# Carried sums of an expert stage added onto the output by five GpSimd transfers between the scatters

## The chip, the cores and the metric

The kernel runs on one core of one Trainium2 chip. The metric is the device time of one execution in microseconds (us). The kernel before took 2507.95 us, the median of 3 runs that lie between 2502.75 and 2509.33.

## What is computed

One layer of a graph transformer on 6250 nodes of 256 features, all in f32. A graph attention part sums over 206250 edges, and a linear attention part runs over all nodes; both are added to the input. Then a mixture of experts follows: each node is sent to its two best of 8 experts (256 to 512 to 256, GELU), weighted by a softmax of the two scores, and added to the node's row. Cut to what matters here:

```python
    x = x + gnn(layernorm(x), edges) + mix(layernorm(x))
    # ffn, on the layer norm of the new x:
    logits = xn @ Wr + br
    top_vals, top_idx = jax.lax.top_k(logits, 2)
    w = softmax(top_vals)
    for e in range(8):
        h = gelu(xn @ W1[e] + b1[e])
        y = y + (h @ W2[e] + b2[e]) * w_full[..., e, None]
    x = x + y
```

## The kernel before

Nodes lie in 49 tiles of 128 rows. A main stage of about 2200 us gathers the rows of the edges' sources (L1262), block by block, and weaves the other parts in between. As soon as a group of tiles has its new rows x, they are stored to `out` and also sent, by expert, into a DRAM tensor `expert_in`. An expert tile is 256 such rows of one expert. The first 28 expert tiles ("carried") are worked off inside the main stage and leave their result rows in a DRAM tensor `y_rows`; `y_at` tells for each node and each of its two choices where its row lies in it (or a row of zeros).

`tail_stage` (L2165) is the last stage, some 290 us, and the change is in it alone. It has T = 28 expert tiles left. Each engine has a hand-written program; the order in which an engine's waits and instructions stand in it is the order in which it runs. Per tile n:

- SP loads the 256 rows (`rows_in`, L2270) and the two weight matrices of the tile's expert (`weights`, L2277 and L2278, 512 KB each), into 3 buffers each. The weights of tile n wait until `down(n - 3)` is done.
- PE transposes the rows (`rows_across`, L2380), multiplies by W1 (`up`, L2392) and by W2 (`down`, L2404), in the order up(n), rows_across(n+1), down(n-1).
- ACT applies GELU (L2359).
- DVE scales the transposed rows (`rows_back`, L2432 to L2436, L681, L682) and makes the result rows `ye` (`result`, L2448, L2450). The result of tile n-1 stands in turn n of DVE's loop. There are 6 buffers for `ye` and 9 for the row numbers.
- GpSimd (POOL) adds the 256 result rows onto `out` in DRAM by two indirect transfers with compute_op add, 128 rows each (`result`, L2327). Two adding transfers must not meet on one row, so each tile's pair waits on the semaphore `added` until the pair before has landed.

Beside the tiles, GpSimd fetches the rows of the carried tiles for the nodes of the first 35 node tiles: two indirect gathers for each node tile t (`early_rows`, L2317), the first choice into `early[t]`, the second into one of GS = 5 buffers `second`. DVE adds the second to the first (`early_sum`, L2453) and counts in `early_done`; the gather of node tile t waits until sum t - 4 is done, because it takes that buffer. Five node tiles are gathered ahead of the first scatter; the others follow in `TILES_AFTER`, one node tile after most scatters. DVE makes its first five sums in turn LAG - 1 = 3.

When all 28 tiles are scattered, an epilogue puts `early` onto the output in five groups of 7 node tiles (896 KB): SP reads the rows of `out` into SBUF (`sums`, L2302), DVE adds (L2480), ACT's queue stores them (L2368).

The stage also carries the last group of node tiles, three of them, through its row steps (`part`, a shared function with numbered steps u; `STEPS` gives each step's tile, the same for all engines): steps 4 to 9 give the new x (ACT scales h by a weight of each row and head, L386; DVE adds, L484, and takes reciprocals; ACT scales again, L395; DVE adds the base, L489), 10 to 12 the normalised rows, 13 to 20 the logits, 29 to 33 the choice and the places. Its rows are then scattered to `expert_in` (L344, `SENDS_AT`), and the tile list for tiles 11 to 27 is made (`tile_list`).

Of the kernel before, what the change touches and what calls it, by code (L numbers as in the profile page):

```python
# [20 lines left out]
P = 128  # L21
# [182 lines left out]
class Round:  # L204


    def __init__(self, i, k=0, t=0, l=0, s=0, m=0, turned=False, spread=False):
        self.first, self.gt = sum(SIZES[:i]), SIZES[i]
        self.k, self.t, self.l, self.s, self.m, self.turned, self.spread = k, t, l, s, m, turned, spread
# [22 lines left out]
def rows_part(g, sems, ps):  # L232
# [239 lines left out]
    def vector(dve, own, r, u):  # L472
# [7 lines left out]
        if u == 5:  # L480
            dve.wait_ge(dev_ready, 3 * r.k + 1)
# [5 lines left out]
        elif u == 7:  # L487
            dve.wait_ge(dev_ready, 3 * r.k + 2)
# [9 lines left out]
        elif u == 11:  # L498
            dve.wait_ge(dev_ready, 3 * r.k + 3)
# [93 lines left out]
def tile_list(dve, own, g, count, tiles, partial):  # L593
# [5 lines left out]
    own.do(dve.tensor_tensor(room[:, :], taken[0:1, :], cap[0:1, :], ALU.subtract))  # L599
    own.do(dve.tensor_scalar(room_i[:, :], room[:, :], float(MT - 1 if partial else 0), None, ALU.add))  # L600
    own.do(dve.tensor_scalar(room_i[:, :], room_i[:, :], MT.bit_length() - 1, None, ALU.arith_shift_right))
    own.do(dve.tensor_copy(room[:, :], room_i[:, :]))
    own.do(dve.tensor_tensor(room[:, :], room[:, :], done[:, :], ALU.subtract))
    own.do(dve.tensor_tensor_scan(upto[:, :], unit[:, :], room[:, :], 0.0, ALU.mult, ALU.add))

    own.do(dve.tensor_scalar(coef[:, :], room[:, :], float(-MT), float(CAP), ALU.mult, ALU.add))
    own.do(dve.scalar_tensor_tensor(out=coef[:, 0:E - 1], in0=done[:, 1:E], scalar=float(MT), in1=coef[:, 0:E - 1],
                                    op0=ALU.mult, op1=ALU.add))
    own.do(dve.scalar_tensor_tensor(out=coef[:, :], in0=done[:, :], scalar=float(-MT), in1=coef[:, :], op0=ALU.mult, op1=ALU.add))
# [12 lines left out]
    own.do(dve.tensor_tensor(done[:, 1:E], done[:, 1:E], upto[:, 0:E - 1], ALU.subtract))  # L622

# [1541 lines left out]
def tail_stage(nc, g):  # L2165
# [11 lines left out]
    GS = 5  # L2177
    AHEAD = 5
    LAG = 4
    GATHERS_IN = [2] * GATHERED_TILES  # L2180
    TILES_AFTER, at_tile = {}, AHEAD
    for n in range(REST - 2):
        work = 0
        most = 4 if n in (2, 5, 8, 11) else 2
        while at_tile < GATHERED_TILES and work + GATHERS_IN[at_tile] <= most:
            work += GATHERS_IN[at_tile]
            TILES_AFTER.setdefault(n, []).append(at_tile)
            at_tile += 1
# [4 lines left out]
    PADS_AT = max(STEPS) + 1  # L2193
# [10 lines left out]
    with ExitStack() as ctx:  # L2204
# [28 lines left out]
        second = after_rows(GS * DIM).rearrange("p (s d) -> p s d", s=GS)  # L2233
# [14 lines left out]
        y_in += [Since(old["mix_loads"], 16 * old["MIX_LOADS"]), Since(sem("y_in"), 0)]  # L2248
        early_done, sum_done = Since(old["gdiag"], 1), Since(old["smax_ready"], 1)
        sums = region[:, 0:GATHERED_TILES * DIM].rearrange("p (i t d) -> p i t d", t=GT, d=DIM)  # L2250
# [4 lines left out]
        out_done = Since(weights_in, 16)  # L2255
        xe_loads = [len(range(i, T, XS)) - (i < 2) for i in range(XS)]
        w_loads = [len(range(i, T, WS)) - (i < 1) for i in range(WS)]
        sums_in = [Since(xe_in[i], 16 * xe_loads[i]) for i in range(XS)]
        sums_in += [Since(w_in[i], 32 * w_loads[i]) for i in range(GATHERED_TILES // GT - XS)]
# [3 lines left out]
        def _(sp):  # L2263
# [35 lines left out]
            sp.wait_ge(added, 32 * T)  # L2299
            sp.wait_ge(ye_ready, T)  # L2300
            for i in range(GATHERED_TILES // GT):
                sp.dma_start(sums[:, i], out[i * GT * P:(i + 1) * GT * P, :].rearrange("(t p) d -> p t d", p=P)).then_inc(sums_in[i].sem, 16)  # L2302
            out_done.wait(sp, 16 * (GATHERED_TILES // GT))

        @block.gpsimd
        def _(pool):
# [5 lines left out]
            def early_rows(t):  # L2312

                if t >= GS:
                    early_done.wait(pool, t - GS + 1)
                for c in range(2 - GATHERS_IN[t], 2):
                    pool.indirect_dma_start(  # L2317
                        out=second[:, t % GS, :] if c else early[:, t, :], out_offset=None, in_=y_rows[:, :],
                        in_offset=bass.IndirectOffsetOnAxis(ap=y_at[:, c, t:t + 1], axis=0)).then_inc(y_in[t % GS].sem, 16)
# [10 lines left out]
            for t in range(AHEAD):  # L2330
                early_rows(t)
            for n in range(T):
# [6 lines left out]
                for t in TILES_AFTER.get(n, ()):  # L2339
# [3 lines left out]
        def _(act):  # L2343
            part.sums(act, last, range(G_HEADS // 2, G_HEADS))
# [8 lines left out]
            for n in range(T):  # L2353
# [8 lines left out]
                for u in STEPS.get(n, ()):  # L2362
# [3 lines left out]
            for i in range(GATHERED_TILES // GT):  # L2366
                sum_done.wait(act, i + 1)
                act.dma_start(out[i * GT * P:(i + 1) * GT * P, :].rearrange("(t p) d -> p t d", p=P),  # L2368
                              early[:, i * GT:(i + 1) * GT, :]).then_inc(out_done.sem, 16)

        @block.tensor
        def _(pe):
# [35 lines left out]
            for n in range(T):  # L2408
                up(n)
                if n + 1 < T:  # L2410
# [3 lines left out]
                for u in STEPS.get(n, ()):  # L2414
# [4 lines left out]
        def _(dve):  # L2419
# [6 lines left out]
            def rows_back(n):  # L2426
                e = dve.value_load(tile_expert[0:1, n:n + 1], min_val=0, max_val=EXPERTS - 1)
                if n >= MS:
                    dve.wait_ge(added, 32 * (n - (MS - 1)))
# [11 lines left out]
            def result(n):  # L2441
# [4 lines left out]
                if n >= YS:  # L2446
                    dve.wait_ge(added, 32 * (n - (YS - 1)))
# [3 lines left out]
            def early_sum(t):  # L2451
                y_in[t % GS].wait(dve, 16 * sum(GATHERS_IN[t % GS:t + 1:GS]))
                dve.tensor_tensor(early[:, t, :], early[:, t, :], second[:, t % GS, :], ALU.add).then_inc(early_done.sem, 1)  # L2453
            rows_back(0)
            for n in range(T):
                if n + 1 < T:
                    rows_back(n + 1)
                if n:
                    result(n - 1)
                for u in STEPS.get(n, ()):  # L2460
                    part.vector(dve, own, last, u)
                if n == max(STEPS):
                    own.do(dve.tensor_copy(pad_at[0:1, :], taken[0:1, :]))
                    dve.sem_inc(pads_ready, 1)
                    tile_list(dve, own, g, LAST_LIST, list_at(g, len(LISTS)), True)
                    dve.sem_inc(pads_ready, 1)
                if n == LAG - 1:
                    for t in range(AHEAD):
                        early_sum(t)
                for t in TILES_AFTER.get(n - LAG, ()):  # L2470
                    early_sum(t)
            result(T - 1)
            for n in range(T - LAG, T):
                for t in TILES_AFTER.get(n, ()):
                    early_sum(t)
# [40 lines left out]
```

## Time and profile before

| | |
|---|---|
| median of 3 runs | 2507.95 us |
| the profiled execution's own time | 2508.31 us |
| its span, first to last instruction | 2506.6 us |
| busy: PE, DVE, ACT, POOL | 67%, 53%, 33%, 71% of the span |
| last stage begins | at 2213.7 us |
| PE's last matmul ends | at 2462.9 us |
| last scatter issued, landed | 2477.8 us, 2478.9 us |
| epilogue | from 2478.9 to 2506.6 us |

An engine's busy time does not tell whether it sets the end. Idle time in front of an instruction has a releaser, which is what it had waited for; "issue" as a releaser means that the profile shows none. For a GpSimd transfer the instruction's own time is the time in which GpSimd writes its descriptors; the data moves afterwards, on 16 DMA engines that it shares with the queues of SP (q1) and ACT (q10). GpSimd's queue is q0. The DMA share is the mean busy share of these 16 engines.

### The profile page before, as it was taken

The numbers are of one execution on the slowest core, as the hardware profiler recorded it, in microseconds if no ns is written. First come the engines' busy times: TensorE is split into PE (matmuls) and PEld (weight loads), VectorE is DVE, ScalarE is ACT, GpSimd is POOL, SyncE is SP. The second block draws the span as 40 slices with busy tenths as digits, with TensorE's granted clock in tenths as the row PEclk, the third lists the DMA queues.
The fourth block names the chain that finished last, engine by engine and source line by source line (L and its number), as shares of the span: only waits on it lengthen the run. The fifth ranks groups of instructions, "written<-read, shape, count | busy, mean of one in ns | idle before, by whom it ended". The sixth has DMA issues, their size and how long they took to land. (4 is left out here: it accounts for less than half of the span.)

```text
span 2506.6 us, 56941 instructions
## 1 busy us (share of the span) xinstructions
PE 1681.1 (67%) x18165; PEld 1346.5 (54%) x18165; DVE 1336.9 (53%) x4612; ACT 824.1 (33%) x2485; POOL 1777.2 (71%) x1803
## 2 busy tenths in 40 slices
PE   5677765666767546566566677776777776758992
PEld 4544444545555435445445456555666565647882
DVE  5644455556666444554644655655666645535443
ACT  3433331223333133143143254245343453422220
POOL 1577777777777777777777776677777777746773
PEclk9787775665666555555555577787797786779996
DMA  9577776645565554576576587588678866667886
GB/s 295 145 197 200 201 193 184 192 116 147 147 182 147 149 134 123 150 202 183 159 197 199 168 255 222 164 253 266 179 233 274 249 176 182 186 189 207 241 242 193
DMA packets 317808, 483.96 MB, mean 193 GB/s; under 512 B 77671, under 2 KB 241593, under 8 KB 312893
## 3 DMA queue, kind: packets, MB, share of 16 engines
q0 software_dynamic: 90960, 240.58, 36.0%
q1 hardware_dynamic: 217420, 231.15, 30.1%
q10 hardware_dynamic: 9120, 8.49, 1.0%
q8 instruction: 149, 2.44, 0.4%
q14 instruction: 159, 1.29, 0.2%
HBM read 403.01 MB, written 110.57 MB: 205 GB/s over the span
## 5 line engine op out<-in xcount | busy, mean ns | idle before, releaser
L1262 POOL DMA_INDIRECT region<-node_table,src_idx x1612 | 1571.8, 975 | 535.8 <-issue 462.9
L1456 PE MATMUL ps_p<-region 128*32 128x65 f32 x12896 | 385.5, 286 | 378.3 <-DVE region L1702 377.6
L1456 PEld LDWEIGHTS ps_p<-region 128*32 128x32 f32 x12896 | 298.0, 149 | 471.4 <-DVE region L1702 452.8
L1325 ACT ACTIVATE region<-ps_s,region 128x128 f32<-128x128 f32 x806 | 251.1, 363 | 474.8 <-PE ps_s L1436 471.0
L1702 DVE TENSOR_TENSOR region<-region,ps_p 128x512 f32<-128x512 f32 x403 | 277.0, 687 | 175.4 <-ACT ps_p L1330 98.6
L1441 PEld LDWEIGHTS ps_s<-region 128*128 128x128 f32 x1612 | 336.7, 274 | 60.1 <-issue 27.3
L1330 ACT ACTIVATE ps_p<-region 128x16 f32<-128x16 f32 x403 | 75.6, 188 | 877.8 <-DVE region L1696 872.6
L1436 PE MATMUL ps_s<-ident,region 128*128 128x128 f32 x403 | 163.0, 404 | 264.5 <-DVE region L1696 260.3
L1441 PE MATMUL ps_s<-region 128*128 128x32 f32 x1612 | 317.8, 331 | 3.2 <-ACT region L1325 2.4
L1695 DVE TENSOR_TENSOR region<-region,ps_s 128x32 f32<-128x32 f32 x403 | 74.7, 185 | 393.7 <-DMA region<-node_table,src_idx 338.8
L1436 PEld LDWEIGHTS ps_s<-ident,region 128*128 128x128 f32 x403 | 94.1, 234 | 288.1 <-DVE region L1696 282.9
L1710 DVE SCALAR_TENSOR_TENSOR acc<-ps_p,region,acc 128x65 f32 x806 | 192.9, 281 | 80.6 <-issue 58.0
L1688 DVE TENSOR_TENSOR region<-bm,drep 128x64 f32<-128x64 f32 x403 | 92.3, 229 | 164.3 <-issue 164.3
L2392 PE MATMUL ps_eu<-region 128*128 128x256 f32 x448 | 112.9, 410 | 22.6 <-DVE region L2436 16.6
L2327 POOL DMA_INDIRECT out_dram<-acc,rows_of x56 | 91.1, 1626 | 39.5 <-issue 37.6
L1685 DVE TENSOR_TENSOR region<-region 128x128 f32<-128x128 f32 x403 | 115.0, 285 | 0.5 <-DVE region L1678 0.3
L2392 PEld LDWEIGHTS ps_eu<-region 128*128 128x128 f32 x448 | 92.0, 208 | 39.4 <-DVE region L2436 18.1
L1472 PE MATMUL ps_x<-region 128*128 128x384 f32 x196 | 102.8, 660 | 0.0
L2317 POOL DMA_INDIRECT acc<-y_rows,acc x70 | 70.8, 1011 | 43.1 <-DVE acc L2453 22.1
L2404 PE MATMUL ps_ey<-region 128*128 128x256 f32 x448 | 101.3, 379 | 0.0
L2359 ACT ACTIVATE region<-ps_eu,b1s 128x256 f32<-128x256 f32 x112 | 46.6, 470 | 146.4 <-PE ps_eu L2392 146.3
L2404 PEld LDWEIGHTS ps_ey<-region 128*128 128x128 f32 x448 | 83.2, 190 | 10.3
(370 smaller groups left out, 2397.4 us busy)
## 6 DMA issues: line engine op xcount, KB each, us to landing
region<-in_W_dram SPq DMA_DIRECT2D x84, 512.0 KB, 5.5
expert_in<-run_rows SPq DMA_DIRECT2D x280, 130.0 KB
region<-node_table,src_idx POOLq DMA_INDIRECT x1612
acc<-in_W_dram SPq DMA_DIRECT2D x28, 512.0 KB
region<-expert_in SPq DMA_DIRECT2D x47, 260.0 KB, 5.1
acc<-base_rows SPq DMA_DIRECT2D x13, 896.0 KB, 7.1
qkv_rows<-region SPq DMA_DIRECT2D x49, 194.0 KB
y_rows<-acc SPq DMA_DIRECT2D x28, 256.0 KB
```

What stands on the lines that cost most here:

```text
L1262: pool.indirect_dma_start(out=rows[:, s, j, :], out_offset=None, in_=table[:, :], in_offset=bass.IndirectOffsetOnAxis(ap=src_idx[:, n * SU ...
L1325: m = act.activation(maskT[:, s % 2, k, :], ps_s[s % 2][:, 0:P], ACT.Copy, scale=here[:, k, at(n)])
L1436: pe.transpose(ps_s[s % 2][:, 0:P], mask[:, n % ML].rearrange("p j w -> p (j w)"), ident[:, :]).then_inc(maskT_ps, 1)
L1441: m = pe.matmul(ps_s[s % 2][:, 2 * P:2 * P + SUB * 8], maskT[:, s % 2, k, :], dsel[:, n % ML, k].rearrange("p j c -> p (j c)"), start=k == ...
L1456: m = pe.matmul(ps_p[s % 2][h * WIN:(h + 1) * WIN, 0:HC], wts[:, s % 2, j, h, :], rows[:, s, j, h * HC:(h + 1) * HC], start=j == 0, stop=j ...
L1472: m = pe.matmul(ps_x[2 + a % 2][:, 0:3 * HID], xT_tiles[:, a % XT, c, :], w_q[:, c, :], start=c == 0, stop=c == KC - 1)
L1685: own.step(dve.tensor_tensor(mask[:, n % ML], bcast(rel[:, bass.ds(n * SUB, SUB)], 2, WIN), bcast(win, 1, SUB), ALU.is_equal))
L1688: own.do(dve.tensor_tensor(dsel[:, n % ML], bcast(bm, 1, 2), bcast(drep[:, bass.ds(c, 2), :], 2, SUB), ALU.mult))
L1702: dve.tensor_tensor(wts[:, s % 2], bcast(mask[:, n % ML], 2, G_HEADS), bcast(ex_ps(s), 3, WIN), ALU.mult).then_inc(w_ready, 1)
L1710: m = dve.scalar_tensor_tensor(out=a, in0=ps_p[s % 2][:, 0:HC], scalar=here[:, k, at(n)], in1=a, op0=ALU.mult, op1=ALU.add)
L2392: m = pe.matmul(ps_u[2 * (n % 2) + f // 2][:, (f % 2) * MT:(f % 2 + 1) * MT], w1s[n % WS][:, c, f * P:(f + 1) * P], xeT[:, n % 2, c, :], s ...
L2404: m = pe.matmul(ps_y[n % 2][:, b * DIM:(b + 1) * DIM], hidT[:, n % 2, c, b * P:(b + 1) * P], w2s[n % WS][:, c, :], start=c == 0, stop=c == ...
```

## The change

Three things are changed in `tail_stage`, with what they need in the shared functions:

1. The epilogue is gone. In its place stands `join(n)` in GpSimd's program, after the scatters of tiles 3, 6, 10, 17 and 24: it waits for 7 more early sums and for the scatters of tile n to land, and issues one plain transfer of 896 KB from `early` onto `out` with accumulation. The next scatter waits for it (`added_by` counts 32 for a tile and 16 for a join).
2. There are 7 buffers `second` instead of 5, and 7 node tiles are gathered ahead of the first scatter. After each of tiles 0 to 5 follow two node tiles, after tiles 6 to 21 one. DVE makes two sums in each turn from 1 to 10, and then one.
3. The row steps of the last group stand at places of their own for each engine. Its two scalings by ACT (steps 4 and 6) become two broadcast multiplications on DVE in steps 5 and 7. SP issues 4 and ACT 12 of the group's 16 loads of sums (8 and 8 before), and the weights of tile 2 are loaded after them. The tile list is made one turn later, in two parts.

```diff
@@ vector, step 5 and 7
-            dve.wait_ge(dev_ready, 3 * r.k + 1)
+            if r.alone:
+                dve.wait_ge(row_in, rows_in_by(r))
+                weight = w_self[:, r.first * G_HEADS:(r.first + n) * G_HEADS].rearrange("p (t h) -> p t h", h=G_HEADS)
+                own.do(dve.tensor_tensor(num, num, bcast(weight, 3, HC), ALU.mult))
...
+            if r.alone:
+                own.do(dve.tensor_tensor(num[:, :, :, 0:F_HEAD], num[:, :, :, 0:F_HEAD], bcast(rl, 3, F_HEAD), ALU.mult))
@@ tail_stage
-    GS = 5
-    AHEAD = 5
-    LAG = 4
+    GS = 7
...
+    for n in range(REST - 4):
+        for _ in range(2 if n < 6 else 1):
...
-    last = Round(EARLY)
-    STEPS = {1: (4, 5, 6, 7, 8, 9), 2: (10, 11, 12), 3: (13, 14), 4: (15, 16, 17, 18, 19, 20), 5: (29, 30), 6: (31, 32, 33)}
+    last = Round(EARLY, alone=True)
+    PE_UP = {4: (15,), 5: (19,), 6: (31,)}
+    PE_DOWN = {3: (13,), 4: (17,)}
+    ACT_STEPS = {3: (10, 12, 13, 14), 4: (18,), 6: (31,)}
+    DVE_ROWS = {2: (7, 8), 3: (11,), 4: (16,), 5: (20, 29), 6: (32,)}
+    DVE_RESULT = {1: (5,), 2: (9,), 5: (30,), 6: (33,)}
+    JOIN_AFTER = (3, 6, 10, 17, 24)
+
+    def added_by(n):
+        return 32 * n + 16 * sum(j < n for j in JOIN_AFTER)
@@ sync
-            loads(2)
+            rows_in(2)
             part.sync(sp, last, 0)
-            part.sums(sp, last, range(0, G_HEADS // 2))
+            part.sums(sp, last, (0,))
+            weights(2)
...
-            sp.wait_ge(added, 32 * T)
             sp.wait_ge(ye_ready, T)
-            for i in range(GATHERED_TILES // GT):
-                sp.dma_start(sums[:, i], out[i * GT * P:(i + 1) * GT * P, :].rearrange("(t p) d -> p t d", p=P)).then_inc(sums_in[i].sem, 16)
-            out_done.wait(sp, 16 * (GATHERED_TILES // GT))
+            sp.wait_ge(added, added_by(T))
@@ gpsimd
             def result(n):
                 pool.wait_ge(ye_ready, n + 1)
                 if n:
-                    pool.wait_ge(added, 32 * n)
+                    pool.wait_ge(added, added_by(n))
...
+            def join(n):
+                i = JOIN_AFTER.index(n)
+                early_done.wait(pool, GT * (i + 1))
+                pool.wait_ge(added, added_by(n) + 32)
+                pool.dma_start(out[i * GT * P:(i + 1) * GT * P, :].rearrange("(t p) d -> p t d", p=P),
+                               early[:, i * GT:(i + 1) * GT, :], accum_op=ALU.add).then_inc(added, 16)
...
-                for t in TILES_AFTER.get(n, ()):
+                for t in TILES_AFTER.get(n, ())[:1]:
+                    early_rows(t)
+                if n in JOIN_AFTER:
+                    join(n)
+                for t in TILES_AFTER.get(n, ())[1:]:
                     early_rows(t)
@@ scalar
-            part.sums(act, last, range(G_HEADS // 2, G_HEADS))
+            part.sums(act, last, range(1, G_HEADS))
...
-            for i in range(GATHERED_TILES // GT):
-                sum_done.wait(act, i + 1)
-                act.dma_start(out[i * GT * P:(i + 1) * GT * P, :].rearrange("(t p) d -> p t d", p=P),
-                              early[:, i * GT:(i + 1) * GT, :]).then_inc(out_done.sem, 16)
@@ vector
+                due = 0 if n == 0 else 2 if n <= 10 else 1
+                for t in range(summed, min(summed + due, GATHERED_TILES)):
                     early_sum(t)
...
-            for i in range(GATHERED_TILES // GT):
-                sums_in[i].wait(dve, 16)
-                e = early[:, i * GT:(i + 1) * GT, :]
-                dve.tensor_tensor(e, e, sums[:, i], ALU.add).then_inc(sum_done.sem, 1)
```

## Rows read from the trace of the kernel before

**Rows 1.** Windows of the last stage; columns as its first line names them
```profile
core 0: us, PE busy (x) PEld busy (x) DVE busy (x) ACT busy (x) POOL busy (x), PEclk, DMA share, GB/s
2243.00:2263.00 20.00, 11.33 (x50) 9.80 (x51) 9.74 (x33) 11.61 (x30) 0.09 (x1) 0.83 0.36 110
2263.00:2343.00 80.00, 69.08 (x306) 59.07 (x305) 37.19 (x138) 16.93 (x37) 57.31 (x47) 0.89 0.85 230
2343.00:2463.00 120.00, 119.63 (x582) 104.49 (x580) 51.27 (x157) 26.84 (x64) 87.76 (x67) 1.00 0.83 227
2463.00:2479.00 16.00, 0.00 (x0) 0.00 (x0) 2.14 (x4) 0.00 (x0) 10.95 (x8) 0.60 0.12 21
2479.00:2507.00 28.00, 0.00 (x0) 0.00 (x0) 10.13 (x5) 0.00 (x0) 0.00 (x0) 0.50 0.96 328
```
**Rows 2.** Chain of work that ended last: start, us, what
```profile
2476.20 2.73 DMA out_dram<-acc,rows_of
...
2483.59 14.03 DMA region<-out_dram
...
2497.64 2.03 DVE acc L2480
```
**Rows 3.** Groups of GpSimd's instructions in the last stage, 2213 to 2480 us
```profile
L2327 POOL DMA_INDIRECT out_dram<-acc,rows_of x56 | 91.1, 1626 | 39.5 <-issue 37.6 <-DVE acc L2450 1.9
L2317 POOL DMA_INDIRECT acc<-y_rows,acc x70 | 70.8, 1011 | 43.1 <-DVE acc L2453 22.1 <-issue 20.4 <-DVE acc L2450 0.3
L344 POOL DMA_INDIRECT expert_in<-acc x14 | 14.8, 1060 | 4.1 <-issue 4.1
```
**Rows 4.** Timeline: start, us, what, idle before and releaser
```profile
2232.67 0.69 DVE L2450 TENSOR_TENSOR acc<-region,gates 128x512 f32<-128x512 f32 x1
2239.30 1.55 POOL L2327 DMA_INDIRECT out_dram<-acc,rows_of  x1 [0.30 <-issue]
2241.29 0.97 DVE L484 TENSOR_TENSOR acc<-acc 128x780 f32<-128x780 f32 x1 [7.93 <-ACT acc L386]
2245.62 0.96 DVE L489 TENSOR_TENSOR acc<-acc 128x768 f32<-128x768 f32 x1 [3.10 <-ACT acc L395]
2262.22 1.76 DVE L2453 TENSOR_TENSOR acc<-acc 128x256 f32<-128x256 f32 x5
2262.91 1.28 POOL L2317 DMA_INDIRECT acc<-y_rows,acc  x1 [22.06 <-DVE acc L2453]
```
**Rows 5.** Timeline later in the stage, tile 12's result and scatter, PE's end
```profile
2357.16 0.69 DVE L2450 TENSOR_TENSOR acc<-region,gates 128x512 f32<-128x512 f32 x1
...
2367.91 1.62 POOL L2327 DMA_INDIRECT out_dram<-acc,rows_of  x1 [0.30 <-issue]
...
2455.82 7.08 PE L2404 MATMUL ps_ey<-region 128*128 128x256 f32 x32
```
**Rows 6.** Time from issue to landing of the scatters (line L2327)
```profile
DMA to landing us min/median/max: 2.7/4.8/8.3
```
**Rows 7.** DMA queues from 2240.9 to 2246 us, GpSimd's after the first scatter
```profile
q0 software_dynamic: 268, 0.26, 36.2%
```
**Rows 8.** DMA queues from 2483.6 to 2497.6 us (in the epilogue)
```profile
q1 hardware_dynamic: 3526, 3.54, 76.3%
```
**Rows 9.** DMA queues from 2340 to 2460 us
```profile
q1 hardware_dynamic: 16001, 19.64, 49.7%
q0 software_dynamic: 6364, 7.87, 34.2%
```
**Rows 10.** GpSimd's plain transfers at the kernel's start: duration ns min/median/max
```profile
L1245 POOL DMA_DIRECT2D w_o<-in_w_out_dram x1: 537/537/537, 9.4 to 9.4; - x1
L1240 POOL DMA_DIRECT2D region<-in_w_qkv_dram x1: 937/937/937, 6.0 to 6.0; - x1
```
**Rows 11.** DMA issues from 2469 to 2479.2 us, the epilogue's first read: KB, us to landing
```profile
region<-out_dram SPq DMA_DIRECT2D x1, 896.0 KB, 5.2
```

More of the change, by code:

```diff
@@ L498, in vector @@
         elif u == 11:
-            dve.wait_ge(dev_ready, 3 * r.k + 3)
+            dve.wait_ge(dev_ready, 1 if r.alone else 3 * r.k + 3)
             own.do(dve.reciprocal(scale, sdev))
@@ L590, in wait, with tile_list @@
         eng.wait_ge(self.sem, self.base + n)
-def tile_list(dve, own, g, count, tiles, partial):
+def tile_list(dve, own, g, count, tiles, partial, parts=(0, 1)):
     taken, cap, done, ramp, unit = (g[k] for k in ("taken", "cap", "done", "ramp", "unit"))
@@ L598, in tile_list @@
     E = EXPERTS
[L599 to L609, printed above, removed]
+    if 0 in parts:
+        rooms_left(dve, own, g, partial)
+    if 1 not in parts:
+        return
     l3 = le[:, 0:count * E].rearrange("p (t e) -> p t e", e=E)
@@ L622, in tile_list, with rooms_left @@
     own.do(dve.tensor_tensor(done[:, 1:E], done[:, 1:E], upto[:, 0:E - 1], ALU.subtract))
+def rooms_left(dve, own, g, partial):
+    taken, cap, done, unit, room, room_i, upto, coef = (g[k] for k in (
+        "taken", "cap", "done", "unit", "room", "room_i", "upto", "coef"))
+    E = EXPERTS
+    own.do(dve.tensor_tensor(room[:, :], taken[0:1, :], cap[0:1, :], ALU.subtract))
+    own.do(dve.tensor_scalar(room_i[:, :], room[:, :], float(MT - 1 if partial else 0), None, ALU.add))
+    own.do(dve.tensor_scalar(room_i[:, :], room_i[:, :], MT.bit_length() - 1, None, ALU.arith_shift_right))
+    own.do(dve.tensor_copy(room[:, :], room_i[:, :]))
+    own.do(dve.tensor_tensor(room[:, :], room[:, :], done[:, :], ALU.subtract))
+    own.do(dve.tensor_tensor_scan(upto[:, :], unit[:, :], room[:, :], 0.0, ALU.mult, ALU.add))
+    own.do(dve.tensor_scalar(coef[:, :], room[:, :], float(-MT), float(CAP), ALU.mult, ALU.add))
+    own.do(dve.scalar_tensor_tensor(out=coef[:, 0:E - 1], in0=done[:, 1:E], scalar=float(MT), in1=coef[:, 0:E - 1],
+                                    op0=ALU.mult, op1=ALU.add))
+    own.do(dve.scalar_tensor_tensor(out=coef[:, :], in0=done[:, :], scalar=float(-MT), in1=coef[:, :], op0=ALU.mult, op1=ALU.add))
 def note_list(dve, own, g, q):
@@ L2176, in tail_stage @@
     MS = YS + 3
-    GS = 5
-    AHEAD = 5
-    LAG = 4
+    GS = 7
     GATHERS_IN = [2] * GATHERED_TILES
[L2181 to L2188, printed above, removed]
-    assert at_tile == GATHERED_TILES
-    last = Round(EARLY)
-    STEPS = {1: (4, 5, 6, 7, 8, 9), 2: (10, 11, 12), 3: (13, 14), 4: (15, 16, 17, 18, 19, 20), 5: (29, 30), 6: (31, 32, 33)}
+    TILES_AFTER, at_tile = {}, GS
+    for n in range(REST - 4):
+        for _ in range(2 if n < 6 else 1):
+            if at_tile < GATHERED_TILES:
+                TILES_AFTER.setdefault(n, []).append(at_tile)
+                at_tile += 1
+    assert at_tile == GATHERED_TILES
+    last = Round(EARLY, alone=True)
[7 more added lines that the diff above has]
+        return 32 * n + 16 * sum(j < n for j in JOIN_AFTER)
     SENDS_AT = 5
-    PADS_AT = max(STEPS) + 1
+    PADS_AT = 7
     assert SENDS_AT < KNOWN - 3 and PADS_AT < KNOWN - 3
@@ L2232, in after_rows @@
             return v if dt == F32 else v.bitcast(dt)
-        second = after_rows(GS * DIM).rearrange("p (s d) -> p s d", s=GS)
+        second = [after_rows(DIM) for _ in range(5)] + [carve(DIM) for _ in range(GS - 5)]
         y_at = g["place_buffers"]["y_at"]
@@ L2247, in tail_stage @@
         y_in = [Since(old["gathered"][i], 64 * len(range(i, BLOCKS, old["SL"]))) for i in (1, 2, 3)]
[L2248 to L2250 removed]
+        y_in += [Since(old["mix_loads"], 16 * old["MIX_LOADS"])] + [Since(sem(f"y_in{i}"), 0) for i in range(GS - 4)]
+        early_done = Since(old["gdiag"], 1)
         xe_in = [sem(f"xe_in{i}") for i in range(XS)]
@@ L2317, in early_rows @@
                     pool.indirect_dma_start(
-                        out=second[:, t % GS, :] if c else early[:, t, :], out_offset=None, in_=y_rows[:, :],
+                        out=second[t % GS] if c else early[:, t, :], out_offset=None, in_=y_rows[:, :],
                         in_offset=bass.IndirectOffsetOnAxis(ap=y_at[:, c, t:t + 1], axis=0)).then_inc(y_in[t % GS].sem, 16)
@@ L2409, in _ @@
                 up(n)
+                for u in PE_UP.get(n, ()):
+                    part.tensor(pe, last, u)
                 if n + 1 < T:
@@ L2452, in early_sum @@
                 y_in[t % GS].wait(dve, 16 * sum(GATHERS_IN[t % GS:t + 1:GS]))
-                dve.tensor_tensor(early[:, t, :], early[:, t, :], second[:, t % GS, :], ALU.add).then_inc(early_done.sem, 1)
+                dve.tensor_tensor(early[:, t, :], early[:, t, :], second[t % GS], ALU.add).then_inc(early_done.sem, 1)
             rows_back(0)
+            summed = 0
             for n in range(T):
```

45 lines of the change are left out of this document (22 added, 23 removed).

## The prediction

> **What bounds the kernel now.** The change touches the last stage only, so I read it backwards from the end. The chain of work that ended last shows a pure sequence: the last scatter lands 2.73 us after its issue at 2476.20, so at 2478.9; then the first read back from `out`, four more behind it (the DMA piece ends at 2497.6), the last DVE sum of 2.03 us, and the last store up to the span's end at 2506.6 [rows 2]. From 2478.9 on it is epilogue and nothing else: 2506.6 - 2478.9 = 27.7 us, with PE and GpSimd at zero and the DMA engines at 0.96 [rows 1].
>
> What sets the 2478.9? The windows make PE look like the bound: 119.63 of 120 us busy from 2343 to 2463 [rows 1]. But PE is done at 2462.9 [rows 5] and GpSimd goes on scattering for 15 us. So I looked at how far GpSimd is behind DVE: the result of tile 12 is ready at 2357.85, its scatter begins at 2367.91, 10.1 us later [rows 5]. GpSimd has a backlog of more than a tile in the middle of the stage. It is GpSimd's own chain that ends last, and PE only just keeps pace with it.
>
> What that chain is made of is in the groups of GpSimd's instructions [rows 3]: busy 91.1 + 70.8 + 14.8 = 176.7 us, idle 39.5 + 43.1 + 4.1 = 86.7 us, together 263.4 us. Idle of 0.30 us stands in front of even an unhindered transfer [rows 4]; 140 of them are 42.0 us. One idle stretch is 22.06 us long: the gather of node tile 5 waits for DVE's first early sum at 2262.22 [rows 4], because DVE makes none before its turn 3. That is 21.8 us above the 0.30. The rest, 86.7 - 42.0 - 21.8 = 22.9 us, are waits of the scatters, most of them for the landing of the pair before: 22.9 / 27 = 0.85 us for each of 27 tiles.
>
> **The change part by part.**
>
> Epilogue removed: the end is now the last landing. -27.7 us. Nothing else stood beside it, so all of it counts.
>
> Early sums from turn 1 on: after the scatters of tile 0 the gather of node tile 7 wants one sum, which DVE makes in turn 1. There DVE has the result of tile 0 done at 2233.36 [rows 4], then step 5, then two sums. Step 5 waits for the group's loads; SP's part of them shrinks from 8 to 4 loads, ACT's grows from 8 to 12, which it issues before its first GELU. Before, ACT scaled (L386) and DVE's sum followed at 2241.29 and 2245.62 after waits of 7.93 and 3.10 us on ACT [rows 4]. Now DVE does both scalings itself, two more instructions of the size of L484 and L489, 0.97 + 0.96 us [rows 4]. Even with the old landing DVE would make its first sums before 2246. GpSimd comes to its node tile 7 only at 2240.85 + 4 x 1.31 = 2246.1: four more gathers stand ahead of the first scatter (a gather costs 1.01 + 0.30 us [rows 3, 4]). The stall goes: -21.8 us. If step 5 were late by some us, the same us come back here. The number of gathers, 70, does not change, so moving them costs GpSimd nothing in sum. Three other engines gain by the moved steps: PE ran at 11.33 of 20 us from 2243 to 2263 [rows 1]. As PE and DVE are not the chain, I count 0 for that; what hides it is GpSimd's backlog, and SP's later load of tile 2's weights, the tile list one turn later and the longer turns of DVE have the same cover, of 10 us and more. Without the cover they would matter by a few us.
>
> Landing waits in the new order: tiles 0, 1, 2, 4 and 5 have two node tiles (5.2 us of gathers) behind their scatters instead of one, which covers the landing, so their 0.85 goes: -4.2 us. Tiles 22 to 26 have none. A pair lands 4.8 us after its second issue in the median [rows 6], of which 1.6 are the issue itself and 0.3 the usual gap: 2.9 us of wait instead of 0.85, 5 x 2.05 = +10.2 us. Together +6.0 us.
>
> Five joins. GpSimd waits until tile n's pair has landed (in the waits counted above), issues the join, and its next scatter waits until the join has landed. So the join is serial: from its issue to its landing GpSimd can at most do other gathers. Only at tile 3 is one left to do (two gathers, 2.6 us); `TILES_AFTER` puts the one node tile of tiles 6, 10 and 17 ahead of the join, and tile 24 has none. With L for one join, from issue to landing plus the gap, the sum is 5 L - 2.6 us. Both sides of `ye` have room: 6 buffers, and DVE's lead is about three turns, set now by the gathers for its sums (turn n sums node tile n + 9, gathered after tile n - 4). Queued behind the join's wait on GpSimd are the next scatter and through it `ye`, the loads and PE; they come to rest behind it and do not stretch it.
>
> The sum without L: -27.7 - 21.8 + 6.0 - 2.6 = -46.1 us, so the time is 2508.3 - 46.1 + 5 L = 2462.2 + 5 L. It breaks even at **L = 9.2 us**. Everything hangs on L, and no row of before shows an adding transfer of 896 KB, so it is put together.
>
> - Issue: 128 rows of 1 KB cost GpSimd 0.54 us, twice as many pieces 0.94 us [rows 10]. The join has 7 x 128 pieces of 1 KB in DRAM: 0.54 + 6 x 0.40 = 2.9 us. Low end 0.9; high end, if an adding piece costs what it costs in a scatter, 7 x 1.6 = 11.4 us [rows 3].
> - Gap and completion: 0.3 us, and 1.1 us from issue end to landing in the last tile's scatter (2.73 - 1.6), which moves next to nothing [rows 2].
> - Movement: after the first scatter GpSimd's queue alone moved 0.26 MB in 36.2% of 5.1 us x 16 engines = 29.5 engine-us [rows 7], 113 us per MB. A plain copy in the epilogue took 0.763 x 14 x 16 = 171 engine-us for 3.54 MB [rows 8], 48 us per MB. Adding costs 2.3 times a copy. 0.917 MB x 113 / 16 = 6.5 us on all 16 engines, alone.
> - Sharing: SP's queue holds the engines 49.7% of the time in the even part of the stage [rows 9]. If that went on at its full pace, 6.5 us become 6.5 / 0.503 = 12.9 us. But PE and with it the weights stand still for part of a join.
>
> Alone L is 2.9 + 0.3 + 1.1 + 6.5 = 10.8 us; under full sharing 17.2. I take 11.5, near the lone end, since the loads behind a join come to rest. 5 x 11.5 - 46.1 = **+11.4 us**: 2508.3 + 11.4 = 2519.7 us for this execution, which itself lies 0.4 us above the median. Forecast: 2520 us, 0.5% slower. Own range 2512 to 2535 (L from 10 to 14.5).
>
> **A rule weighed.** The Trainium skill (DMA: Bandwidth & Descriptors, "Anatomy of one DMA — SWDGE (gpsimd) path") puts a GpSimd transfer at about 2.0 us plus bytes / 436 GB/s and says that many descriptors can be emitted before their cost shows. An estimate by that page is 2.0 + 2.1 = 4.1 us for a join, and 2462.2 + 20.5 = 2483 us. The page's figure is for a transfer that doesn't add; the row for adding transfers above is 2.3 times dearer to move, so I keep my sum and give this way of things a chance as the first rival.
>
> **The rivals.**
>
> 1. A join goes like a copy (faster). One plain 896 KB read with nothing beside it lands in 5.2 us [rows 11]. If a large plain transfer is cut into bigger packets than the scatter's rows, so that adding costs no more than copying, L is 5.2: 2462.2 + 26 = 2488 us. For it: the issue of plain transfers is cheap [rows 10]. Against it: the 113 us per MB. It decides as soon as L is under 7.7 (2500.8 us). Chance 0.22. Its range is 2482 to 2500.
> 2. The joins cost what the rest gives back (no difference). The movement begins while GpSimd still writes descriptors, or the issue costs under 1 us: L from 7.7 to 10, 2501 to 2512, about 2508 us. Chance 0.20.
> 3. A join is dear (slower still). It meets a whole tile's weights each time, or its issue goes row by row: L = 16.6 gives 2545, L = 11.4 + 0.3 + 1.1 + 6.5 = 19.3 gives 2559 us. Against it: rows 10 show plain issues at a third of a scatter's. Chance 0.12.
> 4. The change doesn't do what it says: the 22 us stall stays in another place, since sums wait for gathers that wait for sums, or PE's clock falls in its new idle stretches and results come late (the window from 2243 to 2263 has clock 0.83 and a PE at 57% [rows 1]). With cheap joins that gives back the gain, with my L it adds: 2520 + 22 = 2542 us. Chance 0.04.
>
> **How the numbers follow.** Forecast 0.42, rivals 0.22, 0.20, 0.12, 0.04. About 0.3% (7.5 us, from 2500.5 to 2515.5) is what a measurement of this kernel tells from no change. Faster: rival 1 and a little of 4, 0.24. Within: rival 2 and 0.06 of the forecast, 0.26. Slower: 0.36 of the forecast, rival 3, the rest of 4, 0.50. The range: 2486 to 2546 leaves out the low part of rival 1 and the high part of rival 3.
>
> **What the profile after would show.** Right: no L2302, L2368, L2480; the idle of L2317 on L2453 under 1 us; five GpSimd plain transfers out<-acc, with issue to landing of 10 to 14 us and an idle stretch of 7 us or more in front of the scatters of tiles 4, 7, 11, 18 and 25; PE with idle stretches after them, and the end 1 us after GpSimd's last scatter. Wrong: landings of 5 to 6 us (rival 1); an issue of more than 5 us (rival 3); GpSimd waiting for L2450 (rival 4: PE or DVE have become the chain). The prediction fails as a whole if GpSimd's chain isn't the one that ends last.

## The result and the profile after

The changed kernel took 2534.52 us, the median of 4 executions between 2529.16 and 2535.78, beside 2505.35 us for the kernel before (4 executions): a ratio of 1.011, interval 1.0093 to 1.0127. It is slower, as forecast, and by more: the forecast was 2520 us, and 2534.52 lies 0.5 us inside the end of its own range, 2512 to 2535. Its profiled execution took 2535.18 us, its span is 2533.4 us.

The stage by windows; columns are the window, its length, the busy time of PE, PEld, DVE, ACT and POOL, then PEclk, DMA share and GB/s:

```profile
2246.00:2266.00 20.00, 15.52 (x69) 13.05 (x68) 11.14 (x35) 7.60 (x15) 15.30 (x13) 0.91 0.76 198
2266.00:2346.00 80.00, 68.79 (x331) 58.88 (x329) 37.53 (x140) 18.85 (x42) 46.61 (x38) 0.96 0.93 250
2346.00:2466.00 120.00, 88.41 (x404) 75.94 (x404) 39.55 (x120) 18.44 (x44) 70.05 (x53) 0.87 0.78 195
2466.00:2506.00 40.00, 31.64 (x151) 27.13 (x149) 12.80 (x34) 6.71 (x16) 23.55 (x16) 0.97 0.53 108
2506.00:2533.40 27.40, 0.00 (x0) 0.00 (x0) 0.00 (x0) 0.00 (x0) 9.44 (x6) 0.50 0.26 34
```

Against [rows 1]: the hole in GpSimd's work behind 2243 us is gone. But PE, which ran through 119.63 of 120 us there, is busy for 88.41 of 120 here, and its granted clock averages 0.87 of full speed over this window, where it was 1.00. What PE now waits for shows in the waits (engine, line, waited for: us in total, times, longest):

```profile
ACT region L2384 <- PE ps_eu L2413: 195.3, 50, 16.9
POOL out_dram L2342 <- issue: 85.1, 54, 10.7
...
PE ps_eu L2413 <- DVE region L2459: 36.8, 7, 10.0
...
DVE region L2471 <- DMA out_dram<-acc,rows_of: 14.1, 8, 5.5
```

The last row is the origin: DVE waits for a landed scatter, since all its result buffers stand full in front of GpSimd. PE waits for DVE. GpSimd's groups in the stage (line, engine, operation, names, count | busy us, mean ns | idle before us and releasers) answer to [rows 3]:

```profile
L2342 POOL DMA_INDIRECT out_dram<-acc,rows_of x56 | 92.1, 1644 | 86.8 <-issue 85.1 <-DVE acc L2473 1.7
L2332 POOL DMA_INDIRECT acc<-y_rows,acc x60 | 60.5, 1008 | 18.3 <-issue 18.3
L344 POOL DMA_INDIRECT expert_in<-acc x14 | 15.1, 1080 | 4.1 <-issue 4.1
L2332 POOL DMA_INDIRECT region<-y_rows,acc x10 | 9.9, 993 | 3.0 <-issue 3.0
L2349 POOL DMA_DIRECT2D out_dram<-acc x5 | 9.4, 1874 | 11.2 <-DMA out_dram<-acc,rows_of 5.5 <-DVE acc L2473 5.4 <-issue 0.3
```

The gathers have no wait left but their 0.30 us (18.3 / 60), where one alone waited 22.06 us before [rows 4]. The idle of the scatters has grown from 39.5 to 86.8 us. The timeline of GpSimd says where: each join with the scatter after it (start, us, instruction, idle before).

```profile
2281.04 1.91 POOL L2349 DMA_DIRECT2D out_dram<-acc  x1 [0.29 <-issue]
...
2292.59 1.64 POOL L2342 DMA_INDIRECT out_dram<-acc,rows_of  x1 [7.00 <-issue]
...
2333.02 1.88 POOL L2349 DMA_DIRECT2D out_dram<-acc  x1 [5.35 <-DVE acc L2473]
2343.76 1.66 POOL L2342 DMA_INDIRECT out_dram<-acc,rows_of  x1 [8.86 <-issue]
...
2374.93 1.88 POOL L2349 DMA_DIRECT2D out_dram<-acc  x1 [1.52 <-DMA out_dram<-acc,rows_of]
2387.53 1.66 POOL L2342 DMA_INDIRECT out_dram<-acc,rows_of  x1 [10.73 <-issue]
...
2439.07 1.88 POOL L2349 DMA_DIRECT2D out_dram<-acc  x1 [1.29 <-DMA out_dram<-acc,rows_of]
2450.98 1.65 POOL L2342 DMA_INDIRECT out_dram<-acc,rows_of  x1 [10.04 <-issue]
...
2503.68 1.82 POOL L2349 DMA_DIRECT2D out_dram<-acc  x1 [2.72 <-DMA out_dram<-acc,rows_of]
2513.18 1.65 POOL L2342 DMA_INDIRECT out_dram<-acc,rows_of  x1 [7.67 <-issue]
...
2525.93 1.56 POOL L2342 DMA_INDIRECT out_dram<-acc,rows_of  x1 [0.30 <-issue]
```

From a join's start to the next scatter's start are 11.55, 10.74, 12.60, 11.91 and 9.50 us, 56.3 us in all: this is L of the prediction, the time that one join holds GpSimd's chain, 11.3 on average. Two gathers fill 2.6 us of the first; in the other four GpSimd does nothing. The fifth is the only one beside which no weights are loaded; DMA queues from 2504 to 2513.2 us (packets, MB, share of 16 engines):

```profile
q0 software_dynamic: 912, 0.92, 72.2%
```

The share of busy time, times the length of the window, times 16 engines, over the bytes gives the work per MB: 0.722 x 9.2 x 16 / 0.92 = 116 engine-us per MB, against the 113 that [rows 7] gave for the scatter.

**Where the time is.** I measure the stage from GpSimd's first instruction in it (its `memset`) to the span's end: 292.9 us before (2213.7 to 2506.6) and 316.9 us after (2216.5 to 2533.4), so +24.0 us. The other 2.8 us of the difference between the two profiles lie ahead of the stage. They are no effect of the change: over the 13 profiles of this study the stage begins between 2206.7 and 2217.7 us, in no order by kernel. So below I give the stage's length beside each median; it comes from one execution, the profiled one, which need not be a median one.

### The profile page after: what moved, and what is told of

The parts are those of the page before. It is cut to its first block and busy times, and to the rows that moved or that the text cites. A ratio compares the mean times of both kernels' runs of the same rounds, so it can differ in the third digit from the quotient of the medians.

```text
span 2533.4 us, 56914 instructions
## 1 busy us (share of the span) xinstructions
PE 1693.6 (67%) x18165; PEld 1353.9 (53%) x18165; DVE 1329.9 (52%) x4609; ACT 818.0 (32%) x2461; POOL 1789.5 (71%) x1808
## 5 line engine op out<-in xcount | busy, mean ns | idle before, releaser
L2342 POOL DMA_INDIRECT out_dram<-acc,rows_of x56 | 92.1, 1644 | 86.8 <-issue 85.1
L458 PE MATMUL ps_x<-acc 128*128 128x260 f32 x140 | 74.5, 629 | 8.8 <-ACT region L424 5.0
```

## The experiments

e1 to e4 ran on one chip, e5 to e8 on a second, e9 to e11 on a third. Ratios are against the kernel before on the same chip.

**e1: only the epilogue comes back.** Everything of the change but the joins; SP's reads, DVE's sums and ACT's stores of the old epilogue at the end.

```diff
-    JOIN_AFTER = (3, 6, 10, 17, 24)
+    JOIN_AFTER = ()
...
+            early_done.wait(sp, GATHERED_TILES)
+            for i in range(GATHERED_TILES // GT):
+                sp.dma_start(sums[:, i], out[i * GT * P:(i + 1) * GT * P, :].rearrange("(t p) d -> p t d", p=P)).then_inc(sums_in[i].sem, 16)
...
```

> The changed kernel with its joins taken out and the old epilogue (read, add, store) put back; steps, gathers and early sums stay as changed. Theory (GpSimd's serial chain sets the end, and the joins are what costs): the 22 us stall stays away and the epilogue's 27.7 us come back, so against the kernel before -21.8 + 6 us of landing waits that moved = about 2490 us. Rival (the new places of steps and gathers are themselves what makes the changed kernel slow, by PE's and DVE's waits): no faster than before, 2505 us or more.

Measured: 2489.85 us (2488.87 to 2492.94) beside 2507.22 us, ratio 0.9935, interval 0.9916 to 0.9955. The stage has 279.5 us, 13.4 less than before's. Its GpSimd groups:

```profile
L2352 POOL DMA_INDIRECT out_dram<-acc,rows_of x56 | 90.2, 1611 | 47.9 <-issue 46.6 <-DVE acc L2487 1.4
L2342 POOL DMA_INDIRECT acc<-y_rows,acc x60 | 61.0, 1016 | 18.3 <-issue 18.0 <-DVE acc L2487 0.3
```

So parts 2 and 3 of the change gain about what I had put on them (-21.8 + 6.0 = -15.8), and it is the joins that lose it. This kernel beats both others.

**e2: only the joins.** The kernel before, its epilogue replaced by joins after tiles 6, 11, 16, 23 and 27, where its later sums allow them.

```diff
+    JOIN_AFTER = (6, 11, 16, 23, 27)
...
-            for i in range(GATHERED_TILES // GT):
-                sp.dma_start(sums[:, i], out[i * GT * P:(i + 1) * GT * P, :].rearrange("(t p) d -> p t d", p=P)).then_inc(sums_in[i].sem, 16)
...
+            def join(n):
...
+                if n in JOIN_AFTER:
+                    join(n)
```

> The kernel before with only the epilogue replaced by five joins, after tiles 6, 11, 16, 23 and 27, where its early sums are ready. Theory: -27.7 us for the epilogue, +56 us for five joins of 11.3 us each, +5 us for what GpSimd does after its last transfer, which the epilogue had covered: +33, about 2539 us. Rival (a join can hide in the old order, because there GpSimd has a stall of 22 us anyway): 2520 us or less.

Measured: 2529.91 us (2525.54 to 2538.38), ratio 1.0078, interval 1.0059 to 1.0096; the stage has 319.8 us, 26.9 more than before's, in an execution that was 8 us above the median. Slower without any of the other parts, though 9 us less in the median than expected. Its stall is still there, in the row of its gathers:

```profile
L2318 POOL DMA_INDIRECT acc<-y_rows,acc x70 | 72.3, 1033 | 42.9 <-DVE acc L2460 22.4 <-issue 19.8 <-DMA out_dram<-acc,rows_of 0.6
```

And its joins land as after's do (8.7, 10.6 and 11.0 us there); all issues of their line:

```profile
DMA to landing us min/median/max: 8.8/10.4/11.9
```

**e3: the same transfers without adding.** It moves the same bytes but leaves out the addition, so it does not compute the layer.

```diff
-                               early[:, i * GT:(i + 1) * GT, :], accum_op=ALU.add).then_inc(added, 16)
+                               early[:, i * GT:(i + 1) * GT, :]).then_inc(added, 16)
```

> The changed kernel with its five joins as plain writes of the same 896 KB: the addition is left out, so the rows of 35 node tiles hold the carried sums alone at that point. Theory (adding costs 2.3 times a copy in the DMA engines): a join's landing falls from 10.6 us to 6 to 7, five of them give 20 to 24 us back: 2512 us. Rival (the join is dear by its fixed costs and its place in the queue, or by the waits in front of it): landing stays above 9 us and the time above 2525.

Measured: 2508.8 us (10 executions, 2497.71 to 2518.82), ratio 1.0004, interval 0.9987 to 1.002; stage 299.4 us. Adding alone is worth 26 us by the medians and 17.5 us by the stages (the profiled execution of e3 was its slowest). The five L of e3 are 9.26, 9.21, 9.23, 7.00 and 5.68 us, 40.4 in all, 15.9 less than with adding. The row of the five transfers among GpSimd's groups:

```profile
L2349 POOL DMA_DIRECT2D out_dram<-acc x5 | 5.2, 1037 | 7.9 <-DMA out_dram<-acc,rows_of 7.3 <-issue 0.6
```

Their time from issue to landing:

```profile
DMA to landing us min/median/max: 4.8/7.5/8.4
```

And the DMA queue beside the fifth (2491.7 to 2498.5 us), which again has no weights beside it:

```profile
q0 software_dynamic: 240, 0.92, 39.0%
```

The fifth lands in 4.8 us. 0.390 x 6.8 x 16 / 0.92 = 46 engine-us per MB, as for the epilogue's reads (48). The plain transfer goes out in 240 packets, the adding one in 912, so e3 changes two things. Small packets are not what costs. The epilogue's reads moved 3.54 MB in 3526 packets at 48 engine-us per MB [rows 8], and its plain stores onto `out`, from the same tile and alone on the engines from 2497.6 to 2506.6 us of the kernel before, were packets of 1 KB too:

```profile
q10 hardware_dynamic: 2979, 2.99, 93.5%
```

0.935 x 9.0 x 16 / 2.99 = 45 engine-us per MB. So it is the adding that costs, as far as packets of SP's and ACT's queues stand for those of GpSimd's.

**e4: no join and no epilogue.** The carried sums are not put onto the output at all, so this is not the layer either; it gives the price of what was left out.

```diff
-    JOIN_AFTER = (3, 6, 10, 17, 24)
+    JOIN_AFTER = ()
```

> The changed kernel without the joins and without an epilogue; the carried sums are not added to the output. It gives the price of the joins as a whole. Theory: 5 x 11.3 us from issue to the next scatter and some 5 us of waits that the joins caused in front of themselves and behind: 2534.5 - 61 = 2473 us. Rival (PE and DVE have become the chain): 2490 us or more, with GpSimd waiting for results.

Measured: 2468.85 us (2468.37 to 2471.84), ratio 0.9847, interval 0.9829 to 0.9865; stage 262.7 us. So the joins cost 54.2 us by the stages and 65.7 us by the medians, and the old epilogue 16.8 us by the stages (e1 against e4) and 21.0 by the medians. The rows of the joins themselves give 56.3 - 2.6 = 53.7 us. These stage figures are good to some 7 us: e4's last scatter is issued by 257.7 us after the stage's start and e1's by 250.7, with the same work up to there.

**e5 and e6: the moved row steps alone, the new gathers and sums alone,** both on the kernel before with its epilogue. I ran them because my sum had put the whole gain of e1 on the sums.

```diff
e5 against before
-    last = Round(EARLY)
...
+    last = Round(EARLY, alone=True)
...
+    DVE_ROWS = {2: (7, 8), 3: (11,), 4: (16,), 5: (20, 29), 6: (32,)}
...
-            part.sums(sp, last, range(0, G_HEADS // 2))
+            part.sums(sp, last, (0,))
+            weights(2)
...
e6 against before
-    GS = 5
...
+    GS = 7
...
-                if n == LAG - 1:
...
+                due = 0 if n == 0 else 2 if n <= 10 else 1
...
```

> The kernel before with the row steps in their new places and nothing else: 5 gathers ahead, first sums in turn 3 and the epilogue as before. Theory (the early sums' turn sets GpSimd's stall, and turn 3 comes no earlier with the new steps: 48 us after the stage's start in both): the stall of 22 us stays, 2504 to 2508 us, no difference to before. Rival (the steps bring PE and DVE forward and with them the end): 2498 us or less.

> The kernel before with the new gathers and early sums (7 buffers, two sums a turn from turn 1), the row steps in their old places and the epilogue as before. Theory: DVE is held by steps 4 to 9 until 35 us into the stage, GpSimd asks for the first sum at 33 to 34, so a stall of 2 to 5 us stays and some 20 us less than before are left: 2494 us, 4 above the kernel with both. Rival (the sums need the new steps): the stall is only moved, 2503 us or more.

Measured: e5 2504.3 us, ratio 0.9989, interval 0.9969 to 1.0009, stage 292.3 us (-0.6). e6 2500.83 us, ratio 0.9972, interval 0.995 to 0.9993, stage 289.5 us (-3.4). Both together, e1, give -13.4. e6 is the miss: I had expected 2494 us, with 2503 or more as the rival. The gathers of e5:

```profile
L2346 POOL DMA_INDIRECT acc<-y_rows,acc x70 | 71.7, 1025 | 39.7 <-issue 20.7 <-DVE acc L2494 19.0
```

The scatters and gathers of e6:

```profile
L2348 POOL DMA_INDIRECT out_dram<-acc,rows_of x56 | 90.4, 1615 | 56.9 <-issue 53.0 <-DVE acc L2483 3.9
L2338 POOL DMA_INDIRECT acc<-y_rows,acc x60 | 59.4, 991 | 20.9 <-issue 17.7 <-DVE acc L2486 2.9 <-DVE acc L2483 0.3
```

In e5 GpSimd still waits 19 us for the first early sum, as before. In e6 that wait is down to 2.9 us, but the scatters' idle is 56.9 us instead of 39.5 [rows 3] and instead of e1's 47.9. With the old row steps the results come too late: in the first 50 us PE is busy for 34.76 us in e6 and for 37.78 us in e1, and in the next 50 us for 43.24 and 45.62 us. Windows of e6, columns as above:

```profile
2209.00:2259.00 50.00, 34.76 (x140) 28.65 (x141) 17.49 (x60) 18.80 (x49) 36.16 (x36) 0.80 0.82 244
2259.00:2309.00 50.00, 43.24 (x197) 36.93 (x196) 27.05 (x108) 12.82 (x28) 37.54 (x32) 0.90 0.88 242
```

Windows of e1:

```profile
2208.00:2258.00 50.00, 37.78 (x157) 31.22 (x156) 20.16 (x64) 14.73 (x30) 38.32 (x37) 0.83 0.86 263
2258.00:2308.00 50.00, 45.62 (x221) 39.04 (x221) 30.97 (x120) 12.68 (x27) 40.00 (x33) 0.97 0.94 264
```

The scatters say the same: in before those of tiles 1 to 5 start 7.0 to 12.9 us after their results, in e1 0.9 to 3.7 us, in e6 0.9 to 2.4 us, so without the stall GpSimd waits for results there. So I read two delays in the stage's start that stand over each other, each covering most of what the other's removal gives. That rests on one profile of each kernel. The times alone don't show it: the gains of e5 and e6, 0.11% and 0.28%, are each uncertain by 0.2%, and their sum can't be told from e1's 0.65%.

**e7: e1 with the gathers spread evenly.** If GpSimd were still the chain in the stage's start, fewer gathers ahead of the first scatters' turns would help.

```diff
-        for _ in range(2 if n < 6 else 1):
+        for _ in range(2 if n in (1, 3, 5, 7) else 1):
```

> The changed kernel with the old epilogue, and with the gathers spread: one node tile after each of tiles 0 to 23 and a second one after tiles 1, 3, 5 and 7. Theory: each gather of 2.6 us behind a scatter covers its landing wait, the uncovered tiles 22 to 26 cost 10 us in GpSimd's chain, of which 4 come back early in the stage: 2484 us. Rival (PE, 7.36 us a tile, is by now as late as GpSimd): 2489 us, as without.

Measured: 2494.86 us, ratio 0.9929, interval 0.99 to 0.9957; stage 278.5 us against e1's 279.5. The 2484 us of the theory missed by 11. No gain over e1 (0.9935) can be told, so the rival expectation held: the scatters of tiles 1 to 5 begin 0.9 to 1.6 us after their results, and GpSimd cannot be earlier there.

**e8: the five adding transfers at the very end,** back to back, with no scatter between them.

```diff
-    JOIN_AFTER = (3, 6, 10, 17, 24)
+    JOIN_AFTER = ()
...
+            early_done.wait(pool, GATHERED_TILES)
+            pool.wait_ge(added, added_by(T))
+            for i in range(GATHERED_TILES // GT):
+                pool.dma_start(out[i * GT * P:(i + 1) * GT * P, :].rearrange("(t p) d -> p t d", p=P),
+                               early[:, i * GT:(i + 1) * GT, :], accum_op=ALU.add).then_inc(added, 16)
```

> The changed kernel with its five adding transfers one after another at the very end, without waits between them, all after the last scatter has landed. Theory (a join's price is the DMA engines' work, 113 to 116 us per MB added, and not the waits alone): 4.59 MB x 116 / 16 = 33 us of movement, 2 us until it begins and 1 us of landing: 2468.9 - 4.8 (what GpSimd does after its last transfer, now covered) + 36 = 2500 us, slower than read, add and store (2490) and faster than the joins between the tiles (2534). Rival (what costs is only that each join is waited for): five in flight together move at a copy's speed, 2484 us.

Measured: 2497.66 us (10 executions), ratio 0.9942, interval 0.9911 to 0.9974; stage 285.5 us. The five issues in GpSimd's timeline:

```profile
2465.20 8.85 POOL L2369 DMA_DIRECT2D out_dram<-acc  x5 [1.76 <-DMA out_dram<-acc,rows_of]
```

Their row by line (count: ns min/median/max, first and last start) and their landings:

```profile
L2369 POOL DMA_DIRECT2D out_dram<-acc x5: 1836/3367/4994, 2465.2 to 2469.1; - x5
...
DMA to landing us min/median/max: 8.9/16.5/23.9
```

The queue from 2462 to 2500 us:

```profile
q0 software_dynamic: 4848, 4.59, 78.8%
```

0.788 x 38 x 16 / 4.59 = 104 engine-us per MB. The last one, issued at 2469.1, lands 23.9 us later, so all five are done 27.8 us after the first start: 5.6 us each, since the next one's descriptors are written while one moves. Between the scatters the same five took 56.3 us, 28.5 more. Five like the lone fifth join would take 5 x 9.50 = 47.5 us. So by this estimate some 20 of the 28.5 us come from standing apart, where each pays its issue and its landing by itself, and some 9 from the loads beside the first four.

The expected 2500 us was near, by two errors that partly cancel: 36 us stood there for the movement where 27.8 were needed, and what GpSimd does after its last transfer was taken as covered. It was not, as its queue's closing DRAIN shows, an instruction at the end of the block:

```profile
L2227 POOLq DRAIN  x1: 29426/29426/29426, 2467.1 to 2467.1; - x1
```

It ends at 2496.5 us, 3.5 us behind the last landing.

**e9, e10 and e11: before, after and e1 once more, on another chip.** The kernels are unchanged.

> The kernel before, unchanged, profiled again, to see how steady the length of the last stage is. If the stage's length is steady, 292 to 294 us again from its first GpSimd instruction to the end, and only its start moves (2207 to 2218 us so far in the profiles), then differences of 3 us in it can be read; if it moves by 5 us or more, the kernel with the new sums alone (289.6) can't be told from before.

> The changed kernel, unchanged, profiled again: the stage takes 315 to 319 us again, and the five joins land after 8.7 to 11 us each, if these belong to the kernel and not to one execution.

> The changed steps, gathers and sums with the old epilogue, timed again beside the kernel before over five rounds: 16 us faster than before (2490), stage of 279 to 281 us. If its gain is of the chip or the moment, 2500 us or more.

Measured: before 2501.58 us in one execution (2507.52 is the median of 11 on this chip), stage 293.1 us; after 2533.69 us in one execution, stage 321.5 us, its five L together 56.5 us; e1 in 5 rounds 2493.55 us, ratio 0.994, interval 0.9917 to 0.9964, stage 280.4 us. The sum of L repeats, and so do the stages of before (by 0.2 us) and of e1 (by 0.9 us). After's stage was expected at 315 to 319 us and came out 4.6 us longer than the first time, so a difference like e6's 3.4 us is not safe by itself.

## Why the prediction was right, and where it was not

Direction and mechanism held: GpSimd's chain sets the end, each join stands in it from issue to landing, and five of them cost more than the stall and the epilogue together. The forecast was +11.4 us on the stage; measured were +24.0 and, in the second pair, +28.5. The terms that the forecast lacked, a closing DRAIN (4.7 us) and longer waits of the scatters (8 us), more than doubled it. By its own steps:

- **L.** 56.3 and 56.5 us for five instead of 57.5. The total was right, its parts less so. The issue takes 1.88 us, not 2.9: the pieces of a plain pattern cost less than I drew from two rows. A join beside weights takes more than I left for it: 9.50 us for the lone fifth (forecast alone 10.8), 11.7 on average for the other four. That these two errors cancel is luck. "They come to rest behind it and do not stretch it" did not hold while a join ran: in the windows of the first four (2281 to 2293, 2333 to 2344, 2375 to 2388 and 2439 to 2451 us) PE was busy for 47.6 of 48 us, and SP's queue held the engines for 47 to 58% of the time, where it was 49.7% before [rows 9]. PE's idle stretches came behind the joins. Nor did that sharing stretch a join to the 17.2 us that I had worked out for it: the landings, 8.7 to 11.0 us, lie mostly below the 10 to 14 that I gave as a sign. The 113 us per MB, on which the sum hung, was measured at 116.
- **Epilogue -27.7 us.** This step failed by 4.7 us. "Nothing else stood beside it, so all of it counts" overlooked a closing DRAIN in GpSimd's queue. Before, it ended at 2482.7 us, under the epilogue; after, it is the last thing, to 2533.2 us, with the last scatter landed at 2528.65. "The end 1 us after GpSimd's last scatter" is 5.9 us in truth. Before's row (line, queue, instruction, count: ns, start):

```profile
L2204 POOLq DRAIN  x1: 8106/8106/8106, 2474.6 to 2474.6; - x1
```

After's row:

```profile
L2227 POOLq DRAIN  x1: 8833/8833/8833, 2524.4 to 2524.4; - x1
```

The row starts when its queue reaches it; what counts is its end, 4.8 to 5.7 us after GpSimd's last issue ends in before, after, e1 and e4, which all end with a scatter. It is no fixed time after the issue: with a join as the last transfer it ended 8.1 us after the issue in e2 and 22.5 us after it in e8, which was 1.0 and 3.5 us behind the landing. For e4 the terms with it give -27.7 - 21.8 + 6.0 + 4.7 = -38.8 us, and 2468.85 - 2507.22 = -38.4 were measured; by the stages it is only 262.7 - 292.9 = -30.2, so the close agreement of the medians is in part chance.
- **Stall -21.8, waits +6.0.** -15.8 together; e1 shows -13.4 and -12.7 us by the stages and -17.4 and -14.0 by the medians. The size is right, the reason half wrong. "As PE and DVE are not the chain, I count 0 for that; what hides it is GpSimd's backlog" failed: with the stall gone GpSimd has little backlog in the stage's start, and when the results come counts there, which e6 without the moved row steps shows by its profile (stage -3.4 us instead of -13.4). The sentence on the missing cover was in the prediction; that the change itself takes the cover away was not.
- **Waits of the scatters and ahead of joins.** I had 22.9 + 6.0 = 28.9 us above the usual 0.30. After has 86.8 + 11.2 - 44.3 (idle behind the joins) - 16.8 (the 0.30 of the other 56) = 36.9 us, the second execution of after by the same sum 43.7. The largest one is ahead of the second join, 5.35 us: the pair of tile 6, issued at 2323.48, landed only at 2331.87. GpSimd's queue was not alone in that time: from 2323.5 to 2333 us SP's queue moved 1.54 MB, mostly the weights of one tile and rows of two. Before that, until 2322.0, SP had issued nothing for 17 us, 16.0 of them waiting for the sends, and these stood behind the first join. So what a join holds up can come back as a longer wait of a later one; that this is the cause was read from one trace and not tested. But e4, without joins, has 39.2 us of such waits in its profile, and e1 only 31.1. How much of the 8 to 15 us is due to the joins, and how much differs from one execution to the next, stays open.
- **The sum with measured terms** for after's profile: 2462.2 + 56.3 + 4.7 (DRAIN) + 8.0 (waits) + 0.9 (busy time of the other instructions) + 2.8 (start of the stage) = 2534.9 us; measured 2535.18. As every term is read from this same profile, it shows that none is missing, and nothing more.

**The rivals.** The first, that a join goes like a copy, is half true of the plain form: 46 us per MB, 4.8 us when alone. The adding form is 2.5 times that. From issue to landing the lone plain transfer took 4.8 us, the median of the plain ones is 7.5, and the adding ones took 8.7 and 10.6. An estimate by the fit of the Trainium skill (DMA: Bandwidth & Descriptors, "Anatomy of one DMA — SWDGE (gpsimd) path") is 4.1 us, near the lone plain transfer only. Its sentence that many descriptors can be emitted before their cost shows agrees better than my 2.9 us: 896 plain pieces were written in 1.02 us. The second rival needed an L under 10 on average, and only the lone fifth join was (9.50 us); the third needed over 16, and none was. The fourth, a stall in another place, did not come: the longest gather wait is 0.31 us in after.

**Could a join pay at all?** The epilogue costs 27.7 - 4.7 = 23.0 us, since it covers the DRAIN, and by e1 against e4 even less. Five joins would have to take under (23.0 + 2.6) / 5 = 5.1 us each. Even the plain ones of e3 take 5.7 (the lone one) to 9.3 us, and e3 lies 19 us behind e1. In the epilogue the DMA engines work at 0.96 [rows 1]; between the scatters GpSimd's chain stands still for a join. Back to back at the end, as in e8, five adding transfers cost about what the epilogue does: e8's ratio, 0.9942, can't be told from e1's 0.9935 and 0.994, though its stage is 6.0 us longer (285.5 against 279.5). The version to keep is e1: the moved steps and the early sums with the old epilogue.

## What to carry to other kernels

A transfer that must not overlap its neighbours on one queue costs its whole time from issue to landing in that queue, as often as it is cut; price it by that, and set it against what it replaces only after asking what else that work covered. When a stall is removed, the work that it had covered can become the chain, so two edits can be worth more together than alone: test each alone and both, with enough runs to tell the difference. An adding DMA has to be priced by a row of adding DMAs.

## What the runs showed of the hardware

- Adding onto DRAM took 104 to 116 engine-us per MB in three kernels, for indirect rows and for one plain pattern alike; the same pattern without adding took 46, and plain stores of the ACT queue in 1 KB packets 45. GpSimd's issue of the 896 KB took 1.87 us with adding and 1.04 without.
- Five adding transfers in a row took 5.6 us each, one by one between scatters 11.3 us on average, and 9.50 us where nothing else moved.
- After GpSimd's last transfer its queue ran a DRAIN that ended behind the last landing: by 3.8 us in before, 4.6 in after, 1.0 in e2 and 3.5 in e8. In before, 3.8 us of the epilogue ran beside it.
